# Second attention of a fused two-layer block: scores of eight heads in two neighbouring PSUM banks, probabilities as the stationary operand, values with a column of ones

## The reference

```
x = x + tanh(g_xattn[0]) * attn0(layernorm(x), ctx)      # one head, q = x W.T + b, keys = values = ctx
x = x + tanh(g_ffn[0])   * moe0(layernorm(x))            # 16 experts, top 4, one shared expert
x = x + tanh(g_xattn[1]) * attn1(layernorm(x), ctx)      # 16 heads of 8, below
x = x + tanh(g_ffn[1])   * moe1(layernorm(x))            # 8 experts, top 2

q = (xn @ Wq.T + bq) -> (B, 16, SQ, 8) * 8**-0.5         # attn1; k and v likewise from ctx
scores = einsum('bhqd,bhkd->bhqk', q, k)
ctx_out = einsum('bhqk,bhkd->bhqd', softmax(scores), v)
out = ctx_out.reshape(B, SQ, 128) @ Wo.T + bo
```

## Time and profile before

| | us |
|---|---|
| median of 3 runs | 337.23 (336.18 to 338.31) |
| profiled execution, whole | 339.97 |
| its span, first to last instruction | 337.3 |
| TensorE matmul busy in the span | 296.4 (88%) |
| VectorE busy | 247.9 (73%) |
| ScalarE busy | 165.1 (49%) |
| GpSimd busy | 103.8 (31%) |
| mean granted TensorE clock | 0.969 of 2.4 GHz |

### The profile page before, as it was taken

How to read it: one execution, slowest core, us unless ns; L and a number is a source line. 1 busy time by engine, 2 the same in 40 slices (tenths; PEclk the granted TensorE clock), 3 DMA queues, 4 the chain that set the end, 5 groups by cost and what they waited for, 6 DMA issues and landing times.

```text
span 337.3 us, 5717 instructions
## 1 busy us (share of the span) xinstructions
PE 296.4 (88%) x1488; PEld 222.8 (66%) x1488; DVE 247.9 (73%) x727; ACT 165.1 (49%) x427; POOL 103.8 (31%) x157
## 2 busy tenths in 40 slices
PE   1889879998998999858898898898887999999995
PEld 1677756665766666537787787787874667676662
DVE  2479778976887977654868868868868877958662
ACT  1237653224233242466798797797862233233321
POOL 6216615020055010263529829829401010100000
PEclk9999958999899999987999999999999999999999
DMA  7901104818605125000000000000004233061550
GB/s 216 328 16 38 31 4 153 247 28 256 166 26 176 54 97 157 0 1 0 2 1 3 2 0 0 0 0 1 3 17 154 83 121 116 22 209 36 165 179 31
DMA packets 16279, 26.45 MB, mean 78 GB/s; under 512 B 2789, under 2 KB 5299, under 8 KB 16051
## 3 DMA queue, kind: packets, MB, share of 16 engines
q1 hardware_dynamic: 15448, 24.93, 24.0%
q10 hardware_dynamic: 808, 1.25, 1.3%
HBM read 24.29 MB, written 1.25 MB: 76 GB/s over the span
## 4 chain that ended last, share of the span: by engine, by line
PE 54%; DVE 17%; ACT 8%; DMA 7%; issue 6%; SPq 3%; POOL 2%; DVEq 1%; ACTq 0%; POOLq 0%
PE bank L547 20%; PE Ybank L569 13%; DMA CR<-comb_rows 4%; PE bank L722 4%; ACT PX L977 3%; DVE cmx L1327 2%; DVE xn L1088 2%; PE Tb L471 2%; DMA comb_rows<-ct 2%; DVE st L1074 2%; SPq L295 1%; DMA CB<-in_consts 1%; DVE recT L1343 1%; SPq L302 1%; DVE xl L1094 1%
## 5 line engine op out<-in xcount | busy, mean ns | idle before, releaser
L890 ACT ACTIVATE sg<-bank 128x512 f32<-128x512 f32 x64 | 38.1, 597 | 76.6 <-PE bank L547 59.4
L334 POOL TENSOR_TENSOR rstd<-ve,mhalf 128x4 f32<-128x4 f32 x16 | 16.2, 1011 | 162.2 <-DVE ve L1081 162.2
L1227 DVE TENSOR_TENSOR hb<-sg,CR 128x512 f32<-128x512 f32 x64 | 44.9, 703 | 18.4 <-DMA CR<-comb_rows 8.4
L1220 DVE TENSOR_TENSOR sg<-sg,bank 128x512 f32<-128x512 f32 x64 | 43.5, 680 | 6.7 <-PE bank L547 4.2
L1327 DVE TENSOR_REDUCE cmx<-bank 128x4 f32<-128x308 f32 x64 | 28.3, 472 | 17.5 <-PE bank L695 17.2
L342 POOL TENSOR_TENSOR KS<-kr,CB 128x1232 fp32r<-128x1232 f32 x16 | 36.1, 2260 | 11.3 <-PE bank L695 11.3
L547 PE MATMUL bank<-xh,WBH 128*128 128x512 f32 x68 | 36.2, 533 | 1.2 <-DVE sg L1220 0.6
L547 PE MATMUL bank<-xh,UPH 128*128 128x512 f32 x64 | 36.2, 566 | 0.0
L569 PE MATMUL Ybank<-hb,W2T 128*128 128x512 f32 x64 | 33.5, 604 | 3.1 <-DVE hb L1227 3.1
L569 PE MATMUL Ybank<-hb,downw 128*128 128x512 f32 x64 | 33.0, 599 | 0.4 <-DVE hb L1227 0.3
L977 ACT ACTIVATE PX<-bank,cmx 128x77 f32<-128x77 f32 x128 | 29.4, 355 | 0.0
(11 more groups left out here) (179 smaller groups left out, 612.0 us busy)
## 6 DMA issues: line engine op xcount, KB each, us to landing
CR<-comb_rows SPq DMA_DIRECT2D x64, 128.0 KB, 3.0
CR<-comb_rows SPq DMA_DIRECT2D x32, 256.0 KB, 3.4
VX<-in_vs_seed SPq DMA_DIRECT2D x4, 320.0 KB, 4.6
w13raw<-in_w SPq DMA_DIRECT2D x1, 1088.0 KB, 11.6
X<-in_x SPq DMA_DIRECT2D x4, 256.0 KB, 9.5
upraw<-in_up SPq DMA_DIRECT2D x4, 256.0 KB, 4.7
out_x<-X SPq DMA_DIRECT2D x4, 256.0 KB, 3.6
cT<-in_ctxT SPq DMA_DIRECT2D x4, 154.0 KB, 6.1
```

Source lines behind the costliest of these rows:

```text
L334: nc.gpsimd.tensor_tensor(rstd[:], ve[:], mhalf[:], ALU.pow).then_inc(rstd_rdy, 1)
L890: A(sg[:, k % 2, :], Gb[k % 2][:], ACT.Silu).then_inc(m.s_done, 1)
L1220: V.tensor_tensor(sg[:, k % 2, :], sg[:, k % 2, :], Ub[k % 2][:], ALU.mult).then_inc(m.t2, 1)
L1227: V.tensor_tensor(hb[:, k % 2, :], sg[:, k % 2, :], CR[:, k % RING, :], ALU.mult).then_inc(m.h_done, 1)
```

## The change

- Scores: the four banks 0 to 3 become one tensor S4. A half u (eight heads, two matmuls) lies in two neighbouring banks, and c_max, c_center and the exponential each handle such a half in one instruction of 616 columns; no exponential reads PSUM with a bias any more.
- Mix: pt chunks become the stationary operand, and the values the moving one, read straight from VS, where each head now has HV = 9 columns, the ninth a column of ones (memset once in Vn before the copies to VS). The output bO9 has tokens on the partitions and 16 x 9 columns; it is accumulated over ten chunks onto a matmul with zero weights and zero rows (ZR). VX, its seed, place_values, c_sums and its semaphores go. pt has two buffers.
- Normalization: a reciprocal of 16 numbers and one multiply; c_turn transposes the result, c_turned on ScalarE copies it to OTs, then c_project. All of this comes within the next step.
- Order: the scores of half 1 come after the projection; c_mix is whole and last in the step; ScalarE takes the exponential of half 0 of the next batch ahead of the third eviction; VectorE starts with the normalization of the batch before. The repeats and the query are moved as the diff shows. At the first batch the turn of ysb stands ahead of the mix.
- later_load: the loads of upraw and downw take the places of the seed's.

The first two excerpts are TensorE's c_mix and c_body, the third ScalarE's c_body, the last three VectorE's.

```diff
-            def c_mix(g, t, u, first):
+            def c_mix(g, t, first):
                 n = GB * g + t
-                if u == 0:
-                    pe.wait_ge(c_ev, START + 3 * n + 3)
-                    pe.wait_ge(vx_rdy, n + 1)
-                    if not (first and t == 0):
-                        pe.wait_ge(c_fin, START + n - 1)
-                    if first and t == 1:
-                        pe.wait_ge(x_done, START + 2 * NG)
-                for c in range(u * CU, (u + 1) * CU):
-                    w = chunk_rows(c)
-                    v = (t % 2 * NC + c) * P
-                    i = mm(bOut[t % 2][:, u * P:(u + 1) * P], VX[0:w, v:v + P], pt[0:w, c * P:(c + 1) * P],
-                           start=c % CU == 0, stop=c % CU == CU - 1)
-                if u == NU - 1:
-                    i.then_inc(c_pv, 1)
+                pe.wait_ge(c_fin, START + n)
+                if first and t == 0:
+                    pe.wait_ge(mB.y_cp, START + NG)
+                    pe.wait_ge(in_vs, 16 * len(pieces))
+                mm(bO9, RK[:, 0, 0:4, :].rearrange("p a b -> p (a b)"), ZR[:], start=True, stop=False,
+                   skip_group_check=True)
+                pe.wait_ge(c_ev, START + 3 * n + 3)
+                for c in range(NC):
+                    w, m = chunk_rows(c), chunk_heads(c)
+                    h = c // CU * UH + chunk_head(c)
+                    v = VS[0:w, c, 0:m, bass.ds(n, 1), :].rearrange("p i a d -> p i (a d)")
+                    i = mm(bO9[:, h * HV:(h + m) * HV], pt[0:w, t % 2, c * P:(c + 1) * P], v, start=False,
+                           stop=c == NC - 1, skip_group_check=True)
+                i.then_inc(c_pv, 1)
...
+                    if t < GB - 1:
+                        c_scores(*n1, 0)
+                    c_transpose(g, t, 0)
+                    if t == GB - 1 and not last:
+                        c_scores(*n1, 0)
+                    if before:
+                        c_turn(*before)
+                    if t == GB - 1 and not last:
+                        c_repeat(g + 1, 2)
+                    c_transpose(g, t, 1)
+                    if before:
+                        c_project(*before)
+                    if t < GB - 1:
+                        c_scores(*n1, 1)
+                    elif not last:
+                        c_repeat(g + 1, 3)
...
                     if t == 2 and not last:
                         c_repeat(g + 1, 0)
+                    c_transpose(g, t, 2)
+                    if t == 1:
+                        if last:
+                            m_logits(mD, 0)
+                        else:
+                            c_query(g + 1)
+                    if t == GB - 1:
+                        if last:
+                            m_route_T(mD, 0)
+                        else:
+                            c_scores(*n1, 1)
                     if t == 0 and first:
                         m_turn(mB, NG - 1, Tb)
+                    c_mix(g, t, first)
                     if t == 0:
+                        if first:
+                            pe.wait_ge(x_done, START + 2 * NG)
                         norm_T(2 * NG + 2 + g)
                     if t == 2 and not last:
                         c_repeat(g + 1, 1)
...
             def c_body(g, first, last):
+                    c_copy(g, t, 0, first)
                     if t or not first:
+                        c_turned(*((g, t - 1) if t else (g - 1, GB - 1)))
+                    if t == 3 and not last:
+                        c_repeat(g + 1, 2)
+                    if t == 3 and last:
+                        m_route_tanh(mD, 0)
+                    c_copy(g, t, 1, first)
+                    if ahead:
+                        c_exps(*n1, 0)
+                    if t in (2, 3) and not last:
+                        c_repeat(g + 1, 0 if t == 2 else 3)
+                    c_copy(g, t, 2, first)
...
+            def pair(u):
+                return S4[:, 2 * u * 512:2 * (u + 1) * 512].rearrange("p (s c) -> p s c", s=2)[:, :, 0:HG * S].rearrange(
+                    "p s (h k) -> p s h k", h=HG)
...
             def c_normalize(g, t):
                 n = GB * g + t
+                mixed = bO9.rearrange("p (h d) -> p h d", h=NH)
+                dve.wait_ge(c_pv, START + n + 1)
+                V.reciprocal(rec[:], mixed[:, :, HD]).then_inc(c_rs, 1)
+                dve.wait_ge(c_rs, n + 1)
+                dve.wait_ge(c_ot, START + n)
+                V.tensor_tensor(On[:], mixed[:, :, 0:HD], rec[:].unsqueeze(2).to_broadcast([P, NH, HD]),
                                 ALU.mult).then_inc(c_norm, 1)
...
             def c_body(g, first, last):
+                    if before:
+                        c_normalize(*before)
                     if ahead:
                         c_max(*n1, 0)
+                        c_center(*n1, 0)
+                    else:
+                        route_weights(mD, 0)
+                    if t == 0 and first:
+                        m_update(mB, NG - 1, Tb)
+                    if before:
+                        c_final(*before)
                     if t == 1:
                         norm_lo(2 * NG + 2 + g, g + 1)
                     if ahead:
+                        c_max(*n1, 1)
+                        c_center(*n1, 1)
                     if t == GB - 1 and not last:
                         norm_stats(2 * NG + 3 + g, (g + 2) % NG)
```

More of the change, by code:

```diff
@@ L279, in later_load @@
                 if n < 4:
[L280 to L287, removed]
+                    sp.dma_start(upraw[:, n * GT:(n + 1) * GT], up[:, n * GT:(n + 1) * GT]).then_inc(in_up, 16)
+                elif n < 6:
+                    sp.dma_start(downw[:, 4 * (n - 4):4 * (n - 3), :], down[:, 4 * (n - 4):4 * (n - 3), :]).then_inc(
                         in_up, 16)
@@ L397, in norm_apply @@
                                         ALU.mult).then_inc(xn_rdy, 1)
[L399 to L410, removed]
-                dst = VX[:, at:at + NU * half].rearrange("p (u r) -> p u r", u=NU)[:, :, 0:2 * HD]
-                nc.gpsimd.tensor_copy(dst.rearrange("p u (i d) -> p u i d", i=2), src[:, :, 4, 0:2]).then_inc(vx_rdy, 1)
             def c_body(g, last):
@@ L755, in c_body @@
-                    if end:
+                    before = (g, t - 1) if t else None if first else (g - 1, GB - 1)
+                    if t < GB - 1:
[8 more added lines that the diff above has]
+                    c_transpose(g, t, 1)
@@ L773, in c_body @@
                         c_repeat(g + 1, 1)
-                    if end:
-                        m_gate(mD, 0, 1)
-                        c_project(g, t - 1)
-                    c_mix(g, t, 1, first)
-                    if t == 2 and not last:
-                        c_repeat(g + 1, 2)
             def c_ahead(k):
@@ L792, in c_ahead @@
                     pe.wait_ge(mB.h_done, START + mB.units * (NG - 1) + mB.units)
-                    for s in range(3):
-                        c_scores(0, 0, s, first=True)
+                    for u in range(NU):
+                        c_scores(0, 0, u, first=True)
             m_body(mB, NG - 1, (2 * NG + 1, None, 0), c_ahead)
             pe.wait_ge(wo_rdy, 1)
-            c_scores(0, 0, 3)
             c_body(0, True, False)
@@ L1035, in _ @@
             m_y_copy(m, NG - 1)
-            for s in range(NHG):
-                c_exps(0, 0, s, first=True)
+            for u in range(NU):
+                c_exps(0, 0, u)
             c_body(0, True, False)
@@ L1394, in c_body @@
                         route_pick(mD, 0)
-                    if t == 0 and first:
-                        m_update(mB, NG - 1, Tb)
-                    if end:
-                        c_final(g, t - 1)
             def c_ahead(k):
@@ L1442, in laid_out @@
     across = lambda v: _np.broadcast_to(v.reshape(-1, 1), (P, P))
-    seed = _np.zeros((P, NC * P), _np.float32)
-    for h, c, row, _, n in value_pieces():
-        ones = c * P + (1 - h // UH) * UD + h % UH * HD
-        seed[row:row + n, ones:ones + HD] = 1.0
     heads = _np.zeros((P, HG), _np.float32)
@@ L1468, in laid_out @@
             f['L1_xattn_bq'].reshape(P, 1), f['L1_xattn_bk'].reshape(P, 1), _np.zeros((P, 1), _np.float32),
-            spread(f['g_xattn']), spread(f['g_ffn']), heads], 1),
-        'vs_seed': seed}
+            spread(f['g_xattn']), spread(f['g_ffn']), heads], 1)}
 def kernel(**inputs):
```

225 lines of the change are left out of this document (80 added, 145 removed).

## The result

The changed kernel took 366.21 us in the median of four executions (361.18 to 369.96), the kernel before on the same chip 336.75 (336.18 to 338.31). The forecast was 339.4 us in a range of 329 to 346, so it missed the time and the range both. The profiled execution of the changed kernel took 361.18 us, its span is 359.4; before it was 337.3, so 22 us came in.

The account below looks back on a forecast made before the run. The second attention was taken as bound by a ring of dependences with nearly full engines. Terms -1.5 + 1.0 + 2.3 + 1.5 - 2.5 = +0.8, plus 1.4 for slow hops, +2.2 us: 339.4 us median, range 329 to 346.

Parts of the forecast that it names:

- the ring: Second attention's serial path per batch: mix, normalization, maximum, centring, exponential, third eviction, mix; plain step 5.57 us, group 26.5 against 25.35.
- t=1: Step of a four-batch group with norm_T ahead of the scores and the query ahead of the mix: 6.55 us.
- slow hop: Hop between engines of 0.20 us, as norm_lo to the query, in place of 0.04; one a batch, +1.4 us in all.
- t=3: Step of a group where the copies of repeats 1 and 3 delay scores and third eviction: 7.3 us.
- t=0: First step of a group, where late scores and norm_stats bring VectorE 0.9 us late to the normalization: 6.5 us.
- the beginning: Start of the second attention: the 1.02 us stall for X goes, scores of t=1 start earlier: -1.5 us.
- the remainder of group 3: End of the second attention: +1.5 us up to the last batch, then -2.5 in the last step.
- the last step: Last batch of the second attention: no next maxima, so the ring opens; -2.5 us after router rows take back 0.2.
- A: Rival: third eviction not held by the exponential, TensorE's issue time sets the group, 23.0 us with gaps; 327 us; chance 0.20.
- B: Rival: 616-wide VectorE operations over two banks take 0.94 us in place of 0.785; +4.3 us, 343.7; chance 0.25.
- C: Rival: a narrow mix pass costs by its columns alone, mix 0.5 us, 29 us go; 310 us; chance 0.03.
- D: Rival: ring right, query or repeats (t=1, t=3) fall otherwise, 1 us a group either way; 335.5 to 343.5; 0.52 with forecast.

Follow-up runs that it names:

- a_wide72: Changed kernel with 72 moving columns of a constant tile in each mix pass in place of 18 or 27 (output not the attention's): 343.3 us, ratio 1.015.
- a_order_dup2: Changed kernel with every mix pass computed twice side by side, third transposes ahead of the projection, their eviction ahead of the exponential: 341.96 us, ratio 1.012.

## Why the prediction was wrong

The step that failed is a term that the sum does not have: what the change does to the clock of TensorE was put at nothing, without a reason. It hides in "So the mix costs 20 x 0.11 = 2.2 us" and "The load sets the pace, not the columns". The pace is the load's, and at full clock the mix did take 2.18 us. But the 0.11 came from rows in which the clock was 1.00, and the prediction took it for a property of the pass. The columns that were saved had cost nothing (the mix of 128 columns took 2.15 us before, 187.35 to 189.50) and had held the clock. The prediction used the clock of one window (0.66 at the start of the stage) and never asked whether the change touched it. None of the rivals had it, either: each priced a longer or shorter ring at a fixed clock. With the clock held but for one window (a_wide72) the kernel takes 343.3 us; without, 362.6. So at least 19.3 of the 25.6 us by which the changed kernel is slower are the clock's, and every instruction of TensorE on the ring pays, not the mix alone. In the profiles, groups of 28.15 and 27.81 us at 72 columns become 32.96 and 34.55 (norm_T at 184.39, 217.35 and 251.90).

The ring itself was right in its links and short in its sizes. At full clock, from the first instruction behind a mix to the first behind the next, a_wide72 has for t=1, 2, 3, 0: 7.15, 6.28, 7.79 and 6.93 us, forecast 6.55, 6.15, 7.3 and 6.5. The misses:
- t=1: norm_lo ends 3.88 us after the start of the step (185.59 - 181.71), forecast 3.6, and TensorE is held 0.87 for the query and the zeroing behind it, forecast 0.7, with the slow hop of 0.20 that I had seen.
- t=3: the late scores end later (the maximum starts at 2.06 us, 197.20 - 195.14, forecast 1.84), and the second pair of scores, which begins at 5.15 (200.29), and the zeroing still stand ahead of the mix, whose times were not counted: it starts at 5.59, forecast 5.1.
- t=0: the late norm_stats pushes the mix to 4.64, forecast 4.3.
- Each step: the reciprocal of 16 strided numbers takes 0.26, not 0.18, and from the end of the maximum to the centring pass 0.13 (189.59 + 0.80 to 190.52), not 0.04.

Together 1.65 us a group. Part by part, between the first score matmuls of t=1 of group 0 and of group 3 the kernel before has 158.55 and 234.31 us, a_wide72 154.66 and 238.03, after a stage before it that ended 1.03 us earlier; the last update of X begins at 256.60 and 260.95. So the beginning gave -2.9 us (forecast -1.5), the three rings between +7.6 (forecast +1.0, +2.3, 0.25 for t=0 of group 3, and 12 of the 14 slow hops: +4.75), and the remainder of group 3 +0.6 (forecast +1.25, -2.5 and two hops: -1.05). Sum +5.3, forecast +2.2. In that remainder the saving at the last step came: from the first transposes of the last batch to its update of X 9.4 us (251.59 to 260.95), before 11.3 (245.28 to 256.60), so -2.0, forecast -2.5. What grew is the two steps ahead of it, 13.6 us in place of 11.0 (+2.6, forecast +1.25 and two hops), a part of them at a clock of 0.74 and 0.69 (243 to 249 us). At a held clock the forecast would have been off by 1.1% (343.3 to 339.4), within its range, in part by luck: the beginning gave 1.4 us more than forecast, the rings took 2.9 more.

Rival by rival. A (TensorE takes over, 327): its condition, the third eviction not behind the exponential, did not hold in the changed kernel (0.67 us of wait ahead of the mix) and was made true in a_order_dup2; there the group went to 26.6 us, not 23.0. At t=2 TensorE did take over; the other steps wait 1.14, 1.21 and 1.08 us for norm_lo, the QS copy and the normalization, where the rival had 0.6 a batch. B (two banks cost twice): out, 0.794 and 0.799 us. C (a narrow pass is cheap): out, 0.109 us with 18 or 27 columns. The row that the prediction took from the Trainium skill, "TensorE: Matmul & The Clock Gate", section "Back-to-back issue gap", is the gap without a load; for a stream of loads and matmuls the same section has the spacing set by both, and the trace agrees: each pass here brings a load of its own. The section "HAM oscillation — how this bites in real kernels" of that page of the Trainium skill tells of a clock that falls in waits for transfers. Here it fell with TensorE busy nine tenths of the stretch, so that section alone would not have given the 19 us either. D (1 us a group either way): the ring came out 1.65 a group longer, 0.4 of it in the lump for slow hops.

## What to carry to other kernels

A price per instruction is taken at a clock. When a change takes moving columns out of passes whose pace the weight load sets, it may save no time (2.19 us for 2.15 here) and take the clock away from everything that TensorE does (0.63 to 0.84 for 1.00 here): look at the granted clock beside each busy share, and count what the array moves before and after. Where such columns are free, fill them (with a second copy, if need be; that gave 12.6 us here), and measure a suspected clock effect in both directions, wide in the new kernel and narrow in the old.

When the pace is a ring, work taken off its engines doesn't shorten it; ask which link each wait belongs to, and move the eviction or copy that the ring needs ahead of those that it doesn't.

## What was not expected of the hardware

- The granted clock fell without a pause. With 27 columns in each pass it was 0.59 to 0.68 while TensorE was busy 25.4 to 25.6 of 27 us; with 64 it was 1.00 in the same windows of the same kernel (0.70 in the one ahead of them). At 36 or 54 it was 0.83 to 1.00 in the changed kernel. How much the rest of the work adds stays open.
- The effect is not steady: the changed kernel took 361 to 370 us and the narrowed kernel before 355 to 369, where the kernel before stayed within 336 to 341 beside them.
- Twice the moving columns in a pass cost nothing that shows: 2.32 us for the doubled mix of 20 passes, and 2.35 for the single one. From the first pass to the next instruction a mix takes 2.19 us at 18 or 27 columns, 2.20 at 72, 2.15 at 128 (before) and 2.40 at 144.
- An operation of VectorE over 616 numbers in two banks costs the slope of one bank: 0.794 and 0.799 us, where that slope gives 0.785 (an estimate from the rows of 308 and 512 columns).
